# Rebuilding the quantised attention product of a two-product kernel: column term on TensorE, all four context groups converted before a block's tiles are evicted

## The chip, the cores and the metric

One NeuronCore of a Trainium2 chip runs the whole program. The metric is the device time of one execution in microseconds (us), as the median of several runs. Lower is better. The cores' engines are named as in the profile: PE (TensorE), DVE (VectorE), ACT (ScalarE), POOL (GpSimd) and SP (SyncE, which here only issues DMAs).

## What is computed

For two batches of 1024 tokens with 2048 features each, and a context matrix of 2048 x 2048 per batch:

```
q(v, s, z) = (clip(round(v / s + z), 0, 255) - z) * s
x = x + q(layernorm(x), s1, z1) @ q(ctx, s2, z2)                 # first product
y = layernorm(x)
base  = y @ kernel + bias
A_eff = einsum('bn,nri->bri', gate, lora_A);  B_eff = einsum('bn,nor->bor', gate, lora_B)   # b = 8 groups, n = 16, r = 32
delta = (y @ A_eff.T) @ B_eff.T + (y @ lora_A_shared.T) @ lora_B_shared.T                   # per group of 256 tokens
x = x + base + delta                                             # second product
```

## The kernel before

**Tiles and blocks.** A batch is 8 tiles of 128 tokens (`t`), its 2048 output columns are 4 blocks of 512 (`j`), and the 16 slices of the inner dimension are 4 groups of 4 (`g`). A PSUM bank holds one tile of one block. The program is written by hand, engine by engine, with semaphores; each engine works its own list in order, so the order of the code is the order of the work. Batch 0 runs its first product (blocks 0 to 3), then its second, then batch 1 the same.

**First product.** Both operands are whole numbers in bf16. A context group is 1 MB of fp32: SP loads it into one of two halves of `stage` (L318), which it may do when the group two before has been converted; ACT scales it (L617), DVE rounds it (L1159) and writes it centred into `ring` (L1163, `converted`). `ring` has room for two blocks here. `lhs` holds the quantised and transposed tokens. PE multiplies tile by tile (L841, 16 matmuls a tile); DVE evicts a tile with `evict1` (L1202), which adds it to `x2`. Because the operands are centred, each output needs a term per row and one per column. The row term is added by ACT (`row_terms`, L767). For the column term DVE sums the converted groups (L1175, L1180, L1183), PE sums that over the partitions with a matrix of ones (L853, or L860 for the very first block), ACT copies it out (`column`, L757) and POOL adds it to each tile of `x2` (`adjust`, L477). `evict1` waits for `adjusted`.

**In the first product of batch 0** the low-rank matrices are made too. `a_effective` (L889, 64 fp32 matmuls, printed as 128 records) follows block 0 on PE, `b_effective` (L903, 16 fp32 matmuls) comes ahead of block 3, and ACT copies their results out (L692, L720). DVE finds their largest magnitudes, and those of the first block of `kernel`, to choose powers of two as scales.

**Second product.** `norm2` (L1220) writes the normed tile, ACT and DVE split it into two fp16 parts in `hl` (`split_hi`, `low2` L1226) and SP transposes both into `lhs` (`turn_y`, L310 and L312). PE starts with tiles 0 and 1 together (`base0_pair`) and takes three matmuls a slice (L961 to L963). `lora_in` (L984), `product_p` and `delta` (L972, L973) add the low-rank part. DVE runs `norm2`, `low2` of tile after tile; in batch 0 two `max_of_w` of block 1 (L1339) stand ahead of tile 6's `norm2`, and their loads stand in SP's list behind `load_a(2)`, which waits for `lora_in(1)`.

**Between the batches** the tokens of batch 1 are normed and quantised during batch 0's second product and written to `q_scratch`. In the last block ACT issues their transposes (`turn_next`, L605), each when PE has done with that tile of `lhs`, and `ring` gets free group by group. In this block DVE runs `evict2` of tiles 0 to 4, context groups 0 and 1, tiles 5 to 7, context groups 2 and 3.

## Time and profile before

| | |
|---|---|
| Time, median of 3 runs | 1163.47 us (1163.18 to 1165.22) |
| Profiled execution, its own time | 1165.81 us |
| Its span, first to last instruction | 1164.2 us |
| PE busy | 1013.1 us (87%) |
| DVE busy | 599.5 us (51%) |
| ACT busy | 323.7 us (28%) |
| POOL busy | 247.6 us (21%) |
| Mean granted PE clock | 0.943 of 2.4 GHz |

PE is the engine to watch: the product matmuls are most of the span, and the time to win is where PE stands still or runs at the lower of its two clocks. A matmul of 512 columns shows some 0.38 us in the rows but starts 0.216 us after the one before; 0.43 us at the lower clock.

### The profile page before, as it was taken

What the parts mean: (1) busy time and instruction counts of PE and PEld (TensorE: products, weight loads), DVE (VectorE), ACT (ScalarE), POOL (GpSimd) and SP (SyncE); (2) the same over time, 40 slices, a digit from 0 to 9 for tenths busy, and PEclk for the clock granted to TensorE, in tenths of its full rate; (3) what the DMA queues carried; (4) which work ended last, traced back from release to release, by engine and by line L of the source; (5) the groups of instructions that cost most, each with busy time, mean ns of one, the idle gap of its engine ahead of it and who ended that gap; (6) DMA issues with size and microseconds to landing.
All of it is one profiled execution on the core that took longest, in us unless ns stands there. A gap on an engine that the chain in (4) does not pass through costs nothing.

```text
span 1164.2 us, 12162 instructions
## 1 busy us (share of the span) xinstructions
PE 1013.1 (87%) x4663; PEld 475.3 (41%) x4663; DVE 599.5 (51%) x786; ACT 323.7 (28%) x303; POOL 247.6 (21%) x246
## 2 busy tenths in 40 slices
PE   0388795778968999899999599998999999999995
PEld 0138342233525444344444244444554444444442
DVE  4952775898754546456441567798745114014010
ACT  1872545332210213213211244442213003003000
POOL 1030303351000130140150044440110301301200
PEclk9895797898988999999999799999999999999998
DMA  8872275545664731741759843356683305204010
GB/s 344 246 212 73 73 278 237 150 126 159 131 155 147 260 137 68 248 180 69 233 205 282 251 160 137 134 118 164 136 216 120 125 24 163 76 31 149 9 45 18
DMA packets 131736, 177.24 MB, mean 152 GB/s; under 512 B 104816, under 2 KB 104816, under 8 KB 119408
## 3 DMA queue, kind: packets, MB, share of 16 engines
q1 hardware_dynamic: 102000, 117.99, 34.3%
q0 software_dynamic: 11904, 50.34, 12.4%
q10 hardware_dynamic: 17792, 8.39, 2.9%
q8 instruction: 24, 0.39, 0.1%
q14 instruction: 16, 0.13, 0.0%
HBM read 124.26 MB, written 27.26 MB: 130 GB/s over the span
## 4 chain that ended last, share of the span: by engine, by line
PE 47%; DVE 22%; DMA 9%; ACT 8%; issue 8%; POOL 2%; ACTq 1%; SPq 1%; DVEq 0%; POOLq 0%
PE psum L961 13%; PE psum L962 13%; PE psum L963 13%; DVE stage L1159 4%; DVE ring L1163 3%; ACT x L767 3%; PE psum L984 3%; PE psum L889 2%; DMA xn<-in_x 2%; DMA stage<-in_w 2%; DVE x L1202 2%; DMA bias_sb<-in_bias 2%; POOL x L494 2%; DVE stats L1119 2%; ACT stage L617 2%
## 5 line engine op out<-in xcount | busy, mean ns | idle before, releaser
L961 PE MATMUL psum<-ring,lhs 128*128 128x512 f16 x1024 | 389.9, 381 | 21.8 <-DMA lhs<-hl 16.6
L962 PE MATMUL psum<-ring,lhs 128*128 128x512 f16 x1024 | 389.8, 381 | 0.0
L963 PE MATMUL psum<-ring,lhs 128*128 128x512 f16 x1024 | 389.5, 380 | 0.0
L841 PE MATMUL psum<-ring,lhs 128*128 128x512 bf16 x1024 | 236.0, 392 | 67.9 <-DVE ring L1163 57.1
L841 PEld LDWEIGHTS psum<-ring,lhs 128*128 128x128 bf16 x1024 | 101.6, 100 | 199.2 <-DVE ring L1163 60.8
L961 PEld LDWEIGHTS psum<-ring,lhs 128*128 128x128 f16 x1024 | 100.5, 98 | 145.3 <-issue 19.5
L963 PEld LDWEIGHTS psum<-ring,lhs 128*128 128x128 f16 x1024 | 100.6, 98 | 121.9 <-issue 1.9
L962 PEld LDWEIGHTS psum<-ring,lhs 128*128 128x128 f16 x1024 | 100.5, 98 | 120.4 <-issue 1.4
L1233 DVE SCALAR_TENSOR_TENSOR x<-psum,sc,x 128x512 f32<-128x512 f32 (+1 forms) x64 | 45.4, 747 | 182.3 <-PE psum L973 181.4
L494 POOL TENSOR_TENSOR x<-x,bias_sb 128x512 f32<-128x512 f32 (+1 forms) x64 | 88.5, 1407 | 216.0 <-DVE xn L1220 139.3
L624 ACT ACTIVATE ring<-stage,sc 128x2048 f16<-128x2048 f32 x32 | 63.6, 2000 | 214.1 <-PE psum L963 161.2
L1189 DVE SCALAR_TENSOR_TENSOR ring<-stage,sc,ring 128x2048 f16<-128x2048 f32 x32 | 74.8, 2349 | 78.4 <-ACT ring L624 78.2
L1159 DVE TENSOR_SCALAR stage<-stage 128x2048 f32<-128x2048 f32 x32 | 50.4, 1574 | 82.5 <-ACT stage L617 82.5
L617 ACT ACTIVATE stage<-stage,sc 128x2048 f32<-128x2048 f32 x32 | 65.9, 2086 | 81.7 <-DMA stage<-in_ctx_in 43.0
L500 POOL DMA_DIRECT2D out<-x x48 | 26.6, 554 | 243.5 <-DVE x L1233 238.9
L477 POOL TENSOR_TENSOR x<-x,xn 128x512 f32<-128x512 f32 x32 | 48.3, 1542 | 105.5 <-ACT x L767 98.4
L477 POOL TENSOR_TENSOR x<-x,bias_sb 128x512 f32<-128x512 f32 x32 | 44.5, 1423 | 87.8 <-ACT x L767 87.8
L612 ACT ACTIVATE hl<-xn 128x2048 f16<-128x2048 f32 x16 | 30.6, 1910 | 81.5 <-DVE xn L1220 70.2
L1195 DVE SCALAR_TENSOR_TENSOR b_st<-stage,sc,b_st 64x1024 f16<-64x1024 f32 x16 | 22.8, 1426 | 51.1 <-ACT b_st L631 51.1
L1202 DVE SCALAR_TENSOR_TENSOR x<-psum,sc,x 128x512 f32<-128x512 f32 x64 | 44.8, 743 | 3.5 <-POOL x L477 3.5
L1163 DVE TENSOR_SCALAR ring<-stage 128x2048 bf16<-128x2048 f32 x32 | 44.6, 1393 | 3.2 <-DVE stage L1159 0.5
L1339 DVE TENSOR_REDUCE sc<-stage 128x1 f32<-128x2048 f32 x16 | 36.0, 2278 | 17.3 <-DMA stage<-in_w 17.3
(128 smaller groups left out, 708.8 us busy)
## 6 DMA issues: line engine op xcount, KB each, us to landing
stage<-in_w SPq DMA_DIRECT2D x40, 1024.0 KB, 6.2
stage<-in_ctx_in SPq DMA_DIRECT2D x32, 1024.0 KB, 4.9
out<-x POOLq DMA_DIRECT2D x64, 256.0 KB, 3.6
x<-in_x POOLq DMA_DIRECT2D x8, 1024.0 KB, 14.9
xn<-in_x POOLq DMA_DIRECT2D x8, 1024.0 KB, 7.5
x<-in_x POOLq DMA_DIRECT2D x4, 2048.0 KB, 13.1
lhs<-in_lora_a SPq DMA_DIRECT2D x4, 1024.0 KB, 6.5
lhs<-in_lora_b SPq DMA_DIRECT2D x4, 1024.0 KB, 8.1
```

Source lines behind the costliest of these rows:

```text
L477: pool.tensor_tensor(v, v, col_sb[n % 2], ALU.add).then_inc(adjusted, 1)
L494: pool.tensor_tensor(v, v, bias_sb[:, :], ALU.add).then_inc(biased, 1)
L617: act.activation(s, s, ACT.Relu, bias=Z2, scale=IS2).then_inc(act_conv, 1)
L624: act.activation(ring[:, g, 0, :, :], stage[:, i % 2, :, :], ACT.Copy, scale=of_block(CW0, j)).then_inc(act_conv, 1)
L841: last = pe.matmul(psum[:, t, :], lhs_q[:, k, t * P:(t + 1) * P], ring_q[:, g, j % 2, u, :], start=(k == 0), stop=(k == KT - 1))
L961: pe.matmul(psum[:, t, :], hi, ring[:, g, 0, u, :], start=(kk == 0), stop=False)
L962: pe.matmul(psum[:, t, :], hi, ring[:, g, 1, u, :], start=False, stop=False)
L963: last = pe.matmul(psum[:, t, :], lo, ring[:, g, 0, u, :], start=False, stop=False)
L1159: dve.tensor_scalar(s, s, 255.0, ROUND, ALU.min, ALU.add).then_inc(dve_mid, 1)
L1163: dve.tensor_scalar(ring_q[:, g, j % 2, :, :], s, -(ROUND + CENTRE), None, ALU.add).then_inc(converted, 1)
L1189: dve.scalar_tensor_tensor(out=ring[:, g, 1, :, :], in0=stage[:, half_w(b, g), :, :], scalar=of_block(CW0, j), in1=ring[:, g, 0, :, :], op ...
L1202: dve.scalar_tensor_tensor(out=v, in0=psum[:, t, :], scalar=S12, in1=v, op0=ALU.mult, op1=ALU.add).then_inc(evicted, 1)
```

## The change

**Column term.** POOL's `adjust` is gone. ACT (`column`) and DVE (`column_low`) write the column sums as two fp16 parts into `col_parts`, and PE adds them in PSUM with one more matmul per tile (`column_term`). Tiles 0 to 3 get theirs together after tile 3, in block 0 of batch 0 tiles 0 to 4 after tile 4. Only with it is `psum_full` raised. `evict1` now waits for the row term instead of `adjusted`. In batch 0 the row terms of blocks 1 to 3 are one ACT instruction per tile.

**Low-rank matrices.** Half of `a_effective` runs ahead of block 0, the other half and all of `b_effective` right behind it. Their results go through DRAM scratch (`store_a_part`, `load_gates`); the part for the four gates of a batch is made in block 1 of that batch. The weights of the first block of `kernel` are loaded into free slots of `lhs` for their maxima (`max_of_first_w`).

**Start.** The scales and the gate come in one DMA. Context groups 2 and 3 of block 0 ("head" groups) have buffers of their own, in both batches, and do not use `stage`.

**Orders.** DVE converts all four groups of the next block and then evicts the tiles of this one; `ones`, `turn_next` and the head loads move as the diff shows (`turn_next` from ACT to SP). In batch 0's second product the loads for the two maxima of block 1 come right behind `turn_y(4)`.

```diff
             sp.wait_ge(x_in[1], 16)
-            load_ctx(0, 0, [0, 1])
+            load_ctx(0, 0, [0])
+            load_lora_a(0)
+            load_ctx(0, 0, [1])
+            load_head(0, 2)
+            load_lora_a(1)
+            load_head(0, 3)
             turn_q(0)
             turn_q(1)
-            load_ctx(0, 0, [2, 3])
+            load_lora_a(2)
+            sp.dma_start(ash(0), lora_as).then_inc(sh_in, 16)
             turn_q(2)
             turn_q(3)
-            sp.dma_start(ash, lora_as).then_inc(sh_in, 16)
-            load_lora_a(0)
-            load_lora_a(1)
+            load_lora_a(3)
+            turn_q(4)
+            turn_q(5)
             load_ctx(0, 1, [0, 1])
-            for t in range(4, TILES):
-                turn_q(t)
-            load_lora_a(2)
-            load_lora_a(3)
+            turn_q(6)
+            turn_q(7)
+            load_lora_b(0)
+            load_lora_b(1)
             load_ctx(0, 1, [2, 3])
-            load_ctx(0, 2, range(NG))
+            load_lora_b(2)
+            load_lora_b(3)
             sp.wait_ge(sh_in, 16)
+            sp.wait_ge(csum_full, 1)
             sp.dma_start(bsh, lora_bs.rearrange("r (a o) -> (r a) o", a=P // RANK)).then_inc(sh_in, 16)
-            for c in (0, 1, 3):
-                load_lora_b(c)
+            load_ctx(0, 2, [0, 1])
+            load_gates(0)
+            load_ctx(0, 2, [2, 3])
+            load_first_w(0)
+            load_first_w(1)
             load_ctx(0, 3, range(NG))
-            for n in range(2):
-                sp.wait_ge(a_dram[n], 16 * (NGATE // 2))
-            load_lora_b(2)
+            load_first_w(2)
+            load_first_w(3)
+
+            def turn_next(b, t):
+
+                if t < 2:
+                    sp.wait_ge(turned[t % 2], turns1(b, t) - 16)
+                else:
+                    sp.wait_ge(turned[t % 2], turns1(b, t - 2))
+                sp.wait_ge(base_done, TILES * blk2(b, 0) - TILES + t + 1)
+                sp.dma_start_transpose(lhs_q[:, :, t * P:(t + 1) * P], q_scratch[t]).then_inc(turned[t % 2], 16)
...
-                    load_ctx(b, 0, range(NG))
+                    load_ctx(b, 0, [0, 1])
+                    sp.wait_ge(q_rows, (b + 1) * TILES)
+                    load_head(b, 2)
+                    for t in range(2):
+                        sp.wait_ge(turned[t], turns1(b, t) - 16)
+                    load_head(b, 3)
+                    for t in range(TILES):
+                        turn_next(b, t)
+                    load_gates(b)
                     with sp.Fori(1, NBLK) as j:
-                        ctx_block(b, j, grp1(b, 0, 0), j * NG + grp1(b, 0, 0))
-                else:
-                    w_peaks_block(0)
...
                 turn_y(b, 4)
+                if b == 0:
+                    w_peaks_block(1)
                 load_a(b, 2)
                 turn_y(b, 5)
-                if b == 0:
-                    w_peaks_block(1)
...
-            def adjust(b, j):
-
-                n = b * NBLK + j
-                pool.wait_ge(col_ready, n + 1)
-                for t in range(TILES):
-                    pool.wait_ge(with_row, n * TILES + t + 1)
-                    v = x2[:, t, j * NW:(j + 1) * NW]
-                    pool.tensor_tensor(v, v, col_sb[n % 2], ALU.add).then_inc(adjusted, 1)
...
+                act.wait_ge(rows_ready, b + 1)
+                if b == 0:
+                    ctx_block(b, 1, [0, 1])
+                    row_terms(0, 1)
+                    column(0)
+                    ctx_block(b, 1, [2])
+                    for k in range(2 * KC, 3 * KC):
+                        a_eff_out(k)
+                    ctx_block(b, 1, [3])
+                    for k in range(3 * KC, KT):
+                        a_eff_out(k)
+                    for n in range(8):
+                        b_eff_out(n)
+                    row_terms(1, NBLK)
+                else:
+                    ctx_block(b, 1, [0])
+                    column(0)
+                    ctx_block(b, 1, [1])
+                    act.wait_ge(res_in[0], 16)
+                    row_terms(0, 1)
+                    ctx_block(b, 1, [2, 3])
+                for j in range(1, NBLK):
+                    if j < NBLK - 1:
+                        ctx_block(b, j + 1, [0])
+                    column(j)
+                    if j < NBLK - 1:
+                        ctx_block(b, j + 1, [1])
                     if b:
                         act.wait_ge(res_in[j], 16)
-                    for t in tiles:
-                        if j == 0:
-                            act.wait_ge(rows_ready, TILES // 2 + b if b else t // 2 + 1)
-                        v = x2[:, t, j * NW:(j + 1) * NW]
-                        act.activation(v, v, ACT.Identity, bias=RC[:, t:t + 1]).then_inc(with_row, 1)
-
-                for j in range(NBLK):
-                    column(j)
-                    row_terms(j)
-                    if b == 0 and j == 2:
-                        shared_hi()
-                        for g in range(NGATE):
-                            gate_hi(g)
-                    if j + 1 < NBLK:
-                        ctx_block(b, j + 1, [0, 1])
-                    if b == 0 and j == 0:
-                        for k in range(KT):
-                            a_eff_out(k)
-                    if j + 1 < NBLK:
+                        row_terms(j, j + 1)
+                    if j == 1:
+                        shared_hi(b)
+                        gate_hi(b, 0)
+                        gate_hi(b, 1)
+                    if j < NBLK - 1:
                         ctx_block(b, j + 1, [2, 3])
-                    if b == 0 and j == 2:
-                        for n in range(NBLK * NQ):
-                            b_eff_out(n)
+                    if j == 1:
+                        gate_hi(b, 2)
+                        gate_hi(b, 3)
...
+            def column_term(b, j, tiles):
+
+                n = b * NBLK + j
+                pe.wait_ge(col_ready, n + 1)
+                for t in tiles:
+                    pe.matmul(psum[:, t, :], ones[:, :], col_parts[:, n % 2, :], start=False, stop=True).then_inc(psum_full, 1)
...
             def first_block():
 
                 half = TILES // 2
+                a_effective(0)
+                a_effective(1)
                 for g in range(NG):
-                    pe.wait_ge(converted, grp1(0, 0, g) + 1)
+                    ring_ready(0, 0, g)
                     for t in range(half):
                         if g == 0:
                             tile_start(0, 0, t)
                         group1(0, t, g)
-                first_column_sum()
+                column_sum(0, 0)
                 for t in range(half, TILES):
                     tile_start(0, 0, t)
                     for g in range(NG):
                         group1(0, t, g)
+                    column_term(0, 0, range(half + 1) if t == half else [t])
+                a_effective(2)
+                a_effective(3)
+                for n in range(8):
+                    b_effective(n)
...
                         group1(j, t, g)
-                    if t == 0:
+                    if t == (0 if j else 2):
                         column_sum(b, j)
+                    if t >= TILES // 2 - 1:
+                        column_term(b, j, range(t + 1) if t == TILES // 2 - 1 else [t])
...
+            def column_low(b, j):
+
+                n = b * NBLK + j
+                v = col_parts[P // 2:P, n % 2, :]
+                dve.wait_ge(col_hi, n + 1)
+                dve.scalar_tensor_tensor(out=v, in0=psum[P // 2:P, CB, :], scalar=D1[P // 2:P, :], in1=v,
+                                         op0=ALU.mult, op1=ALU.subtract).then_inc(col_ready, 1)
...
             def evict_and_convert(b, j):
 
+                last_first = 4 if b == 0 and j == 0 else 0
+                if j == 0:
+                    row_terms(b)
                 ctx_group(b, j + 1, 0)
+                column_low(b, j)
                 ctx_group(b, j + 1, 1)
-                for t in range(4):
+                for t in range(last_first):
                     evict1(b, j, t)
-                ctx_group(b, j + 1, 2)
-                for t in range(4, 6):
+                if j == 1:
+                    shared_low(b)
+                    gate_low(b, 0)
+                    gate_low(b, 1)
+                for g in range(2, NG):
+                    ctx_group(b, j + 1, g)
+                if j == 1:
+                    gate_low(b, 2)
+                    gate_low(b, 3)
+                for t in range(last_first, TILES):
                     evict1(b, j, t)
-                ctx_group(b, j + 1, 3)
-                for t in range(6, TILES):
-                    evict1(b, j, t)
...
                 for j in range(NBLK - 1):
-                    if b == 0 and j == 2:
-                        power_a()
-                        a_low()
                     evict_and_convert(b, j)
                     if b == 0 and j == 0:
-                        peak_a()
+                        peak_a(2)
+                        peak_a(3)
+                        peaks_a()
+                        power_a()
+                        peaks_b()
+                    if b == 0 and j == 1:
+                        max_of_first_w(0)
+                    if b == 0 and j == 2:
+                        for g in range(1, NG):
+                            max_of_first_w(g)
+                        all_of_w(0)
+                        power_b()
 
                 j = NBLK - 1
-                if b == 0:
-                    peaks_b()
-                    max_of_w(0, 0)
-                    max_of_w(0, 1)
                 early_stats2(b, 0)
+                column_low(b, j)
                 evict1(b, j, 0)
                 late_stats2(b, 0)
                 if b == 0:
-                    max_of_w(0, 2)
+                    product_scale(0)
+                early_stats2(b, 1)
+                norm2(b, 0)
                 evict1(b, j, 1)
-                norm2(b, 0)
-                stats2(b, 1)
-                if b == 0:
-                    max_of_w(0, 3)
-                    all_of_w(0)
+                late_stats2(b, 1)
                 low2(b, 0)
...
+                    for t in range(2):
+                        evict2(b, NBLK - 1, t)
+                    for g in range(2, NG):
+                        head_group_mid(b + 1, g)
+                    for t in range(2, 5):
                         evict2(b, NBLK - 1, t)
                     for g in range(2):
                         ctx_group(b + 1, 0, g)
-                    for t in range(5, TILES):
+                    evict2(b, NBLK - 1, 5)
+                    for g in range(2, NG):
+                        head_group_end(b + 1, g)
+                    for t in range(6, TILES):
                         evict2(b, NBLK - 1, t)
-                    for g in range(2, NG):
-                        ctx_group(b + 1, 0, g)
+                    for g in range(NG):
+                        add_group(b + 1, 0, g)
```

Three places in the lists of the engines show what moves.

PE, batch 0, block 0 and what follows it, before (`pats_sb` is the gate pattern, so these rows are `a_effective`):

```order
L841 MATMUL psum<-ring,lhs 128x512 x64
L860 MATMUL psum<-ring,ones_b 128x512 x16
L841 MATMUL psum<-ring,lhs 128x512 x64
L889 MATMUL psum<-pats_sb,lhs 128x64 x64
L841 MATMUL psum<-ring,lhs 128x512 x16
```

And of the change (L1001 is `a_effective`, L978 `column_term`, L1015 `b_effective`):

```order
L1001 MATMUL psum<-pats_sb,lhs 128x64 x32
L943 MATMUL psum<-ring,lhs 128x512 x64
L969 MATMUL psum<-ring,b_st 128x512 x16
L943 MATMUL psum<-ring,lhs 128x512 x16
L978 MATMUL psum<-bias_sb,ones 128x512 x5
L943 MATMUL psum<-ring,lhs 128x512 x16
...
L1001 MATMUL psum<-pats_sb,lhs 128x64 x32
L1015 MATMUL psum<-lhs,pats_sb 128x512 x16
```

Half of `a_effective` stands first, `b_effective` has come forward from block 3, and behind tile 4 PE needs the column sums before it may go on to tile 5.

DVE, batch 0, the stretch in which block 2 is evicted and block 3 converted, before:

```order
L1159 TENSOR_SCALAR stage<-stage 128x2048
L1163 TENSOR_SCALAR ring<-stage 128x2048
L1175 TENSOR_TENSOR xn<-ring 128x2048
L1202 SCALAR_TENSOR_TENSOR x<-psum,sc,x 128x512 x4
L1159 TENSOR_SCALAR stage<-stage 128x2048
L1163 TENSOR_SCALAR ring<-stage 128x2048
L1175 TENSOR_TENSOR xn<-xn,ring 128x2048
L1202 SCALAR_TENSOR_TENSOR x<-psum,sc,x 128x512 x2
```

And of the change, from the second group on (L1353 is `evict1`):

```order
L1279 SCALAR_TENSOR_TENSOR bias_sb<-psum,sc,bias_sb 64x512
L1293 TENSOR_SCALAR stage<-stage 128x2048
L1297 TENSOR_SCALAR ring<-stage 128x2048
L1326 TENSOR_TENSOR xn<-ring 128x2048
...
L1326 TENSOR_TENSOR xn<-xn,ring 128x2048
L1331 TENSOR_TENSOR xn<-xn 128x1024
L1334 TENSOR_TENSOR xn<-xn 128x512
L1353 SCALAR_TENSOR_TENSOR x<-psum,sc,x 128x512 x8
L1513 TENSOR_REDUCE sc<-lhs 128x1 x3
```

The eight evictions have moved behind the last conversion and the sums; a new small instruction (L1279, `column_low`) stands behind the first conversion.

SP, batch 0's second product, between the transposes of tiles 4 and 5, before:

```order
L310 DMA_TRANSPOSE lhs<-hl 128x16x128
L312 DMA_TRANSPOSE lhs<-hl 128x16x128
L402 DMA ap_st<-a_scratch 128x2048
L310 DMA_TRANSPOSE lhs<-hl 128x16x128
L312 DMA_TRANSPOSE lhs<-hl 128x16x128
L370 DMA stage<-in_w 128x2048 x2
```

And of the change (L449 loads the weights, L481 is `load_a`):

```order
L338 DMA_TRANSPOSE lhs<-hl 128x16x128
L343 DMA_TRANSPOSE lhs<-hl 128x16x128
L449 DMA stage<-in_w 128x2048 x2
L481 DMA ap_st<-a_scratch 128x2048
L338 DMA_TRANSPOSE lhs<-hl 128x16x128
L343 DMA_TRANSPOSE lhs<-hl 128x16x128
```

The two weight loads have moved ahead of `load_a(2)` and of tile 5's transposes.

## Rows read from the trace of the kernel before

**Rows 1.** The page's first line

```profile
span 1164.2 us, 12162 instructions
```

**Rows 2.** Stages: us, busy of PE, PEld, DVE, ACT, POOL, clock, DMA share, GB/s

```profile
0.00:38.50 38.50, 0.00 (x0) 0.00 (x0) 20.95 (x55) 14.44 (x12) 5.34 (x16) 1.00 0.84 300
38.50:84.30 45.80, 36.34 (x144) 14.70 (x144) 31.40 (x55) 37.24 (x33) 8.37 (x7) 0.89 0.88 257
84.30:120.40 36.10, 27.54 (x128) 27.39 (x129) 9.58 (x9) 9.75 (x17) 3.44 (x2) 0.54 0.17 60
...
187.10:225.70 38.60, 18.47 (x33) 5.25 (x34) 30.03 (x29) 17.97 (x22) 17.28 (x13) 0.73 0.60 204
...
253.70:266.60 12.90, 0.00 (x0) 0.01 (x1) 12.14 (x14) 5.26 (x4) 4.53 (x2) 0.66 0.59 102
...
651.50:697.80 46.30, 32.81 (x135) 13.58 (x134) 27.80 (x27) 17.84 (x15) 13.82 (x11) 0.82 0.65 210
...
727.90:757.90 30.00, 28.14 (x130) 12.39 (x129) 22.64 (x22) 13.74 (x13) 11.84 (x8) 1.00 0.40 144
...
785.90:789.60 3.70, 0.05 (x1) 0.00 (x0) 3.70 (x3) 0.00 (x0) 0.00 (x0) 1.00 0.86 155
```

**Rows 3.** PE's waits: releaser, us in total, times, longest

```profile
PE psum L841 <- DVE ring L1163: 57.1, 7, 38.5
...
PE psum L972 <- DVE ap_st L1248: 16.5, 3, 13.5
```

**Rows 4.** DVE at the start: start us, us, instruction, [idle before]

```profile
14.01 0.06 DVE L1068 MEMSET sc<- 128x1 f32 x1 [14.01 <-DMA sc<-in_z]
```

**Rows 5.** DMA issues by line: KB each, median us from issue to landing

```profile
stage<-in_ctx_in SPq DMA_DIRECT2D x32, 1024.0 KB, 4.9
...
lhs<-hl SPq DMA_TRANSPOSE x40, 4.6
...
pats_sb<-in_gate SPq DMA_DIRECT2D x1, 4.0 KB, 1.8
```

**Rows 6.** PE in order of time, batch 0 and the start of batch 1

```profile
92.15 27.54 PE L889 MATMUL psum<-pats_sb,lhs 128*128 128x64 f32 x128 [7.92 <-DVE x L1202]
...
198.93 12.58 PE L903 MATMUL psum<-lhs,pats_sb 128*64 128x512 f32 x24 [11.92 <-DVE x L1202]
...
664.49 1.89 PE L841 MATMUL psum<-ring,lhs 128*128 128x512 bf16 x4 [11.09 <-DVE ring L1163]
```

**Rows 7.** DVE in order of time, batch 1, block 1

```profile
718.61 2.72 DVE L1202 SCALAR_TENSOR_TENSOR x<-psum,sc,x 128x512 f32<-128x512 f32 x4
721.25 1.22 DVE L1159 TENSOR_SCALAR stage<-stage 128x2048 f32<-128x2048 f32 x1
...
723.84 1.23 DVE L1175 TENSOR_TENSOR xn<-xn,ring 128x2048 f16<-128x2048 f16 x1
```

**Rows 8.** ACT in order of time, batch 1, block 1

```profile
702.31 5.00 ACT L767 ACTIVATE x<-x,sc 128x512 f32<-128x512 f32 x8
...
722.61 2.10 ACT L617 ACTIVATE stage<-stage,sc 128x2048 f32<-128x2048 f32 x1 [1.72 <-DMA stage<-in_ctx_in]
```

**Rows 9.** DVE in order of time, batch 0's second product

```profile
330.76 2.29 DVE L1339 TENSOR_REDUCE sc<-stage 128x1 f32<-128x2048 f32 x1 [12.08 <-DMA stage<-in_w]
```

**Rows 10.** SP's DMA issues in order of time: the start, and batch 0's second product

```profile
11.25 0.80 SPq L318 DMA_DIRECT2D stage<-in_ctx_in  x2
...
311.41 1.99 SPq L312 DMA_TRANSPOSE lhs<-hl  x1
...
324.82 1.61 SPq L370 DMA_DIRECT2D stage<-in_w  x2
```

**Rows 11.** ACT's DMA issues between the batches

```profile
648.31 11.39 ACTq L605 DMA_TRANSPOSE lhs<-q_scratch  x2
```

**Rows 12.** DVE in order of time, batch 1, block 3

```profile
764.64 0.75 DVE L1202 SCALAR_TENSOR_TENSOR x<-psum,sc,x 128x512 f32<-128x512 f32 x1 [0.20 <-POOL x L477]
...
782.58 2.40 DVE L1226 TENSOR_TENSOR hl<-xn,hl 128x2048 f16<-128x2048 f32 x1
```

534 lines of the change are left out of this document (309 added, 225 removed).

## The prediction

> **What bounds the kernel now.** I read the page's first line [rows 1], then windows at the stage boundaries [rows 2], then PE's waits [rows 3], then the timelines around them. In the second product PE runs at 0.216 us a matmul with few gaps; the time to win lies elsewhere. Batch 0's first product reaches from 38.5 to 266.6 us, 228 us, where 512 product matmuls are 110.5 us. The rest is: an idle start of 38.5 us, `a_effective` with the stall ahead of it (36.1 us in which PE is busy 27.5, at a clock of 0.54), `b_effective` with its stalls (38.6 us, of which PE is busy 18.5), and 12.9 us before the second product, when the clock has dropped as well [rows 2]. In batch 1, block 0 takes 46.3 us instead of 27.8, and a later block 30.0 [rows 2]. The largest waits are on DVE's conversions, and 13.5 us in one piece on `product_p` [rows 3].
>
> The base is the profiled execution, 1165.8 us with a span of 1164.2; it is 2.3 us above the median 1163.5, so I add 1165.8 - 1164.2 - 2.3 = -0.7 to a span. Times below are us from the span's start. The change is followed stage by stage, since in each the last wait is another.
>
> **Start.** DVE stands until 14.01, for a scale that lands late [rows 4]. One parameter DMA like the gate's, which took 1.8 us [rows 5], ends that wait; then x tile 1 binds, whose landing lets SP go at 11.25 [rows 10]. The first norm comes some 6.6 us earlier. Against that, SP now puts 6 MB (two context groups, two head groups, two `lora_a` parts) ahead of the first transpose, where it put 2 MB; with x that is 14.7 MB (14 of 1.05). The first stretch moved 300 GB/s at a DMA share of 0.84 [rows 2], so 357 if always busy: 41 us, ending near 44. I take the first transpose as held behind these loads, landing at 46 instead of some 36. ACT's quantising of tile 2 waits for it, and so do all later tiles.
>
> The Trainium skill, page "DMA: Bandwidth & Descriptors", section "Queues, rings and completion order", says that an engine takes one row's descriptors in ring order and alternates between rows. By that rule x on POOL's queue goes on while the transpose waits behind SP's loads; the sum would be the one I use.
>
> DVE's list then runs unbroken (statistics 2.5 a tile, conversions 1.2 + 1.2, `a_eff_out` and two maxima, some 6 in all, new here). Tile 7 is quantised near 84, when PE had finished block 0 before (84.3 [rows 2]). Now comes the new stall. The row terms wait for all 8 tiles; ACT then does two conversions (2.1 each), eight row terms (5.0) [rows 8] and `column`, DVE `column_low`: 84.4 + 4.1 + 5.0 + 0.7 + 0.5 = 94.7. PE, done with tile 4 near 75, waits there about 20 us. Five column terms, three tiles and their terms are 56 matmuls, 12.1 us, plus 2.3 at the lower clock: block 0 ends at 109 (before 84.3).
>
> **Low-rank work.** `a_effective` costs 0.215 us a record (27.54 / 128 [rows 6]); half of its 128 now run in the idle start, 64 remain: 13.8, to 123. `b_effective` is still 32 records at 0.524 (12.58 / 24 [rows 6], the first of them at the lower clock), 16.8 us; it waits some 1 us for tile 4's eviction, which is behind the fourth conversion, and ends near 140. Its ACT copies fall from 16 to 8. Block 1 starts at 140 and finds its groups converted.
>
> The Trainium skill, page "TensorE: Matmul & The Clock Gate", Part 1, says that activity releases the throttle. Busy 27.5 of 36.1 us these small matmuls sat at a clock of 0.54 [rows 2], so the row wins; at the full clock the 64 records would be 6.9 us, and the sum 7 less.
>
> **Blocks 1 to 3, batch 0.** A block is now 128 product matmuls, 8 column terms and a sum: 137 x 0.216 = 29.6 (64 terms in all, +13.8 us, where POOL's additions cost PE nothing by themselves). In block 1 ACT first does the wide row terms, 8 x 1.5 = 12.3 (three times 0.625, less overhead), then a conversion and `column`: col_ready at 157.9, when PE has waited 3.9. DVE does the low-rank parts of four gates between conversions (6 x 0.75), so its evictions start at 174.6; PE starts block 2 at 175.3 and waits 1.1 for the last eviction, as the column sum uses bank 7. Block 3 starts at 206 (before 225.7) and ends at 235.6.
>
> **Evict after all four conversions.** In a steady block started at T: conversion 0 by T+3.5, `column_low` T+5, conversion 1 T+9.4; groups 2 and 3 are loaded once 0 and 1 are converted (4.9 us to land [rows 5]), scaled (2.1 [rows 8]) and done with their sums by T+22.5. Eight evictions at 0.68 [rows 7] begin then; bank 0 is free at T+23.2 and PE wants it at T+29.6. The order alone costs nothing, with 6.4 us in hand. The 0.45 us of stall per block (30.0 against 29.6) goes.
>
> **Last block.** `column_term` holds the first `psum_full` until after tile 3, T+14.9, where the first eviction was at 764.64, T+6.7 [rows 12]. From there `norm2` and `low2` of two tiles are DVE work without a gap, 20 us (764.64 to 785.0 [rows 12]). So the second product starts at T + 14.9 + 20 + 4.4 for the transpose = T+39.2 instead of T+31.7 (757.9 to 789.6 [rows 2]); in batch 0, with the scale's small steps, T+40.5 = 246.5. **Batch 0's first product: -20.1 us** (266.6 to 246.5).
>
> **Second product, batch 0.** DVE waits 12.08 us for a weight load [rows 9] that SP issues at 324.82, though its buffer is free before. Behind tile 4's transpose (issued 311.41 [rows 10]) it lands by 319.6 and 322; two maxima end at 324.3 instead of 335.6, and `product_p` comes 11.4 earlier. PE's 13.5 us wait [rows 3] shrinks to 2.1, and with it go 2 us of lower clock: **-13.4**.
>
> **Batch 1.** The head groups are ready, so the 11.09 us wait of [rows 6] and two small ones after it, 13.5 in all, go. But PE comes to `column_term` at T+13.8, and col_ready needs ACT's `column`, which stands behind the first load of block 1. SP issues that load only after `turn_next(7)`, whose issue ended at 659.7 on ACT [rows 11], and the gate load: 661, landing with 2.3 MB at about 668.5, scaled 670.6, `column` 671.8, DVE's conversion and `column_low` 674. PE stops from 665.3 to 674, 8.7 us, and loses 2.3 at the lower clock. Block 0 becomes 40.4 instead of 46.3 (-5.9), blocks 1 and 2 -0.9, block 3 with its gap +7.3, clock +0.6: **+1.1**.
>
> Sum of the span: 1164.2 - 20.1 - 13.4 + 1.1 = 1131.8; less 0.7, 1131 us.
>
> **The rivals.**
> *The transposes are not held* (0.13). Plain rotation between transfers would land the first transpose at 34; median landing of transposes is 4.6 [rows 5], though none stood behind 4 MB. Everything up to block 3 comes 9 us earlier: 1122. The small records at the full clock (0.04) would give 1124.
> *More late loads* (0.17). The 168 us up to block 1 of batch 0 are a chain of ACT, SP and DVE with little slack; `load_lora_b(2)` blocks SP until `a_effective` is half done. If groups 2 and 3 and the gate load each come 5 us late, `b_effective` and block 1 move by 10, and batch 1's stall by 4: 1145. The DMA shares of 0.84 and 0.88 at the start [rows 2] speak for it, the shares of 0.17 to 0.6 later against.
> *Slower: the late evictions become the chain* (0.07). Place: each of five steady blocks. A conversion group late by L costs max(0, L - 6.4) per block, and the whole passes the gain of 33 from L = 13. That takes loads of 11 us instead of 4.9 for both pairs; DMA share is 0.40 there [rows 2], which speaks against. At L = 15 it gives 1131 + 43 = 1174.
> *The waits only move* (0.03): the 20 us stop after tile 4 grows to 50 as ACT's list is longer than I count, and 1163 comes out.
>
> **How the numbers follow.** My forecast (0.56) has a range of its own, 1122 to 1140: 5 us either way for the copy of `b_effective` and the clock, 4 for the start. With rivals 1 and 2 the range is 1116 to 1150. A measurement tells 0.2%, 2.3 us. Faster 0.90, within 0.03, slower 0.07.
>
> **What would show it.** Right: PE stops after tile 4 of block 0 for about 20 us on DVE's `column_low`; `a_effective` records at 0.215 us; evictions of a block in one run of eight that ends before PE needs bank 0; DVE's wait for the weight load under 3 us; a stop near 9 us at `column_term` in batch 1's block 0. Wrong: the first transpose landing before 38; a wait for `evicted` at tile starts in every block; base0 of batch 1 more than 42 us after block 3's start.

## The result, and the profile after

The changed kernel takes 1130.2 us (median of 4 runs, 1125.9 to 1131.7), the kernel before 1163.3: a ratio of 0.971, with an interval of 0.968 to 0.975. In a second job with six more runs it took 1131.8 us (1125.9 to 1134.0), ratio 0.9717 (0.9689 to 0.9745). The forecast was 1131, with a range of 1116 to 1150.

The profiled execution is the fastest of its kernel (1125.9 us). The top of its page:

```profile
span 1124.3 us, 12189 instructions
PE 1015.2 (90%) x4727; PEld 477.5 (42%) x4727; DVE 585.0 (52%) x794; ACT 310.9 (28%) x265; POOL 161.8 (14%) x187
```

PE's waits, to be read against [rows 3]: releaser, us in total, times, longest. The wait for `ring`, 57.1 us with the idle start in it, is gone: the idle start now stands in the first wait of `a_effective` (L1001), and the column's low half (L1279) is the new one. That on the product (L1095) has fallen from 16.5 to 6.0.

```profile
PE psum L978 <- DVE bias_sb L1279: 27.1, 3, 18.0
PE psum L1001 <- DMA lhs<-in_lora_a: 23.5, 1, 23.5
PE psum L1084 <- DMA lhs<-hl: 17.9, 2, 9.7
...
PE psum L1095 <- DVE ap_st L1405: 6.0, 3, 3.1
PE psum L943 <- DVE x L1353: 4.8, 2, 4.4
```

Windows by stage, columns as in [rows 2]: block 2 of batch 0; the gap before the second product; then batch 1's block 0 and its last gap.

```profile
175.50:206.70 31.20, 31.20 (x137) 13.76 (x138) 26.60 (x29) 7.18 (x5) 0.00 (x0) 0.95 0.31 119
...
236.40:246.10 9.70, 0.03 (x1) 0.01 (x1) 9.63 (x12) 1.51 (x2) 1.58 (x2) 0.70 0.72 145
...
617.40:654.20 36.80, 31.38 (x139) 13.55 (x136) 23.01 (x25) 15.84 (x14) 2.00 (x3) 0.95 0.85 285
...
744.00:752.20 8.20, 0.32 (x2) 0.00 (x0) 8.13 (x9) 0.26 (x2) 2.42 (x2) 0.80 0.85 162
```

The timeline of PE in batch 0's first product, with the idle time and its releaser in brackets. The 64 records of `a_effective` at 107.12 take 7.25 us; both `column_term` stops and the eviction wait at the start of block 2 are here. The last line is from batch 1: the column sum of its block 1 waits for the last eviction of block 0.

```profile
93.20 2.32 PE L978 MATMUL psum<-bias_sb,ones 128*128 128x512 f16 x5 [18.04 <-DVE bias_sb L1279]
...
107.12 7.25 PE L1001 MATMUL psum<-pats_sb,lhs 128*128 128x64 f32 x64
...
119.08 16.53 PE L1015 MATMUL psum<-lhs,pats_sb 128*128 128x512 f32 x32 [4.71 <-DVE x L1353]
...
153.62 1.04 PE L978 MATMUL psum<-bias_sb,ones 128*128 128x512 f16 x4 [3.97 <-DVE bias_sb L1279]
...
175.47 5.28 PE L943 MATMUL psum<-ring,lhs 128*128 128x512 bf16 x16 [4.45 <-DVE x L1353]
...
246.13 0.59 PE L1084 MATMUL psum<-ring,lhs 128*128 128x512 f16 x1 [9.69 <-DMA lhs<-hl]
...
658.91 0.38 PE L963 MATMUL psum<-xn,ones 128*128 128x512 f16 x1 [1.07 <-DVE x L1353]
```

By large stages, each from a timeline (starts of the first matmuls of a product):

| Stage | before | forecast | after | after, second profile |
|---|---|---|---|---|
| to batch 0's second product | 266.6 | 246.5 | 246.1 | 250.6 |
| second product, batch 0 | 384.9 | 371.5 | 371.3 | 374.4 |
| first product, batch 1 | 138.1 | 139.2 | 135.0 | 135.0 |
| second product, batch 1 | 374.6 | 374.6 | 371.8 | 372.5 |
| span | 1164.2 | 1131.8 | 1124.3 | 1132.4 |

Two profiles of the same kernel differ by 8 us, half of it before 250 us. So an effect below some 4 us is not told here from one profile of each kernel, unless two profiles agree up to the place of the edit.

### The profile page after: what moved, and what is told of

The parts are those of the page before. It is cut to its first block, busy times and chain, and to the rows that moved or that the text cites. A ratio compares the mean times of both kernels' runs of the same rounds, so it can differ in the third digit from the quotient of the medians.

```text
span 1124.3 us, 12189 instructions
## 1 busy us (share of the span) xinstructions
PE 1015.2 (90%) x4727; PEld 477.5 (42%) x4727; DVE 585.0 (52%) x794; ACT 310.9 (28%) x265; POOL 161.8 (14%) x187
## 3 DMA queue, kind: packets, MB, share of 16 engines
q1 hardware_dynamic: 119040, 126.64, 37.9%
## 4 chain that ended last, share of the span: by engine, by line
PE 60%; DVE 14%; DMA 10%; ACT 6%; issue 5%; SPq 3%; POOL 1%; DVEq 0%; POOLq 0%; ACTq 0%
PE psum L1084 15%; PE psum L1085 15%; PE psum L1086 15%; PE psum L943 11%; DMA stage<-in_w 2%; PE psum L1107 2%; DMA stage<-in_ctx_in 2%; ACT x L850 1%; DVE x L1353 1%; DVE stats L1245 1%; DVE ring L1340 1%; DMA lhs<-hl 1%; DMA bias_sb<-in_bias 1%; ACT stage L696 1%; SPq L333 1%
## 5 line engine op out<-in xcount | busy, mean ns | idle before, releaser
L1084 PEld LDWEIGHTS psum<-ring,lhs 128*128 128x128 f16 x1024 | 100.5, 98 | 143.8 <-issue 22.2
L943 PEld LDWEIGHTS psum<-ring,lhs 128*128 128x128 bf16 x1024 | 102.2, 100 | 138.9 <-issue 12.9
L586 POOL TENSOR_TENSOR x<-x,bias_sb 128x512 f32<-128x512 f32 (+1 forms) x64 | 91.3, 1452 | 187.8 <-DVE xn L1375 113.7
L696 ACT ACTIVATE stage<-stage,pats_sb,sc 128x2048 f32<-128x2048 f32 x28 | 58.2, 2087 | 57.8 <-DMA stage<-in_ctx_in 57.0
L1293 DVE TENSOR_SCALAR stage<-stage 128x2048 f32<-128x2048 f32 x28 | 34.3, 1225 | 44.0 <-ACT stage L696 43.8
L1353 DVE SCALAR_TENSOR_TENSOR x<-psum,sc,x 128x512 f32<-128x512 f32 x64 | 44.0, 743 | 14.5 <-PE psum L978 14.3
L1001 PE MATMUL psum<-pats_sb,lhs 128*128 128x64 f32 x128 | 21.4, 348 | 31.0 <-DMA lhs<-in_lora_a 23.5
L978 PE MATMUL psum<-bias_sb,ones 128*128 128x512 f16 x64 | 21.8, 414 | 27.1 <-DVE bias_sb L1279 27.1
L1218 DVE BATCH_NORM_STATS2 stats<-xn 128x6 f32<-128x512 f32 x32 | 19.8, 681 | 46.7 <-DMA xn<-in_x 46.6
L1383 DVE TENSOR_TENSOR hl<-xn,hl 128x2048 f16<-128x2048 f32 x16 | 36.7, 2292 | 6.7 <-DMA lhs<-hl 4.5
## 6 DMA issues: line engine op xcount, KB each, us to landing
x<-in_x POOLq DMA_DIRECT2D x4, 2048.0 KB, 13.8
```

The lines of the kernel that those rows point to most:

```text
L586: pool.tensor_tensor(v, v, bias_sb[:, :], ALU.add).then_inc(biased, 1)
L696: act.activation(s, s, ACT.Relu, bias=Z2, scale=IS2).then_inc(act_conv, 1)
L943: last = pe.matmul(psum[:, t, :], lhs_q[:, k, t * P:(t + 1) * P], ring_q[:, g, j % 2, u, :], start=(k == 0), stop=False)
L1084: pe.matmul(psum[:, t, :], hi, ring[:, g, 0, u, :], start=(kk == 0), stop=False)
L1293: dve.tensor_scalar(s, s, 255.0, ROUND, ALU.min, ALU.add).then_inc(dve_mid, 1)
L1353: dve.scalar_tensor_tensor(out=v, in0=psum[:, t, :], scalar=S12, in1=v, op0=ALU.mult, op1=ALU.add).then_inc(evicted, 1)
```

## Experiments

The time of the kernel before lies between 1161.8 and 1163.4 (medians) in the three jobs. Times are medians of 5 runs or more; "r" is the ratio to the kernel before, measured beside it, to be held against 0.9717. The changed kernel itself was measured again in the first job only, so for the other two the ratio is the safer comparison. The interval of an r is some 0.003 to either side, so a difference of two of them is known to about 5 us: a gain of 7 us is clear of that, one of 4 us is not and needs the traces beside it.

| Kernel | us | r, interval |
|---|---|---|
| changed kernel | 1131.8 | 0.9717, 0.9689 to 0.9745 |
| old interleaving in it | 1122.4 | 0.9653, 0.9630 to 0.9676 |
| weight loads late again | 1138.8 | 0.9793, 0.9769 to 0.9817 |
| last block's terms after tile 1 | 1125.6 | 0.9681, 0.9655 to 0.9707 |
| head loads behind two transposes | 1123.6 | 0.9682, 0.9656 to 0.9708 |
| batch 1's column first | 1128.9 | 0.9735, 0.9705 to 0.9764 |
| gates 2, 3 behind evictions | 1121.3 | 0.9657, 0.9628 to 0.9687 |
| the same, and 8 evictions in block 0 | 1122.0 | 0.9671, 0.9643 to 0.9699 |
| interleaving + column first | 1123.4 | 0.9653, 0.9620 to 0.9686 |
| five edits together | 1115.0 | 0.9583, 0.9552 to 0.9615 |
| kernel before, late evictions | 1182.1 | 1.0152, 1.0116 to 1.0187 |
| kernel before, early weight loads | 1150.9 | 0.9904, 0.9875 to 0.9933 |

The yardstick of the first job:

> The changed kernel itself once more, as the yardstick for the other kernels of this job: 1130 us, between 1126 and 1132, 0.971 of the kernel before. All theories expect the same.

It gave 1131.8 us, as all theories had it.

**1. The order of the title, undone.**

```diff
-                for g in range(2, NG):
-                    ctx_group(b, j + 1, g)
+                cuts = [last_first, last_first, TILES] if last_first else [4, 6, TILES]
+                for t in range(last_first, cuts[0]):
+                    evict1(b, j, t)
+                ctx_group(b, j + 1, 2)
+                for t in range(cuts[0], cuts[1]):
+                    evict1(b, j, t)
+                ctx_group(b, j + 1, 3)
...
-                for t in range(last_first, TILES):
+                for t in range(cuts[1], TILES):
                     evict1(b, j, t)
```

> VectorE's old interleaving put back into the changed kernel (four evictions behind conversion 1, two behind conversion 2, two behind conversion 3) in every block but the first of batch 0. Theory A (the late evictions cost nothing, 6.4 us in hand per block): within 2 us of the changed kernel, and PE's waits at tile starts stay near zero in both. Rival B (the late order brings something of its own, the folded sums 1.4 us earlier per block, since they no longer stand behind evictions): 1 to 2 us slower for each of five blocks, +5 to +9, seen as waits of PE on the column sum. Rival C (evicting late costs, because VectorE idles ahead of conversions): 3 to 8 us faster.

Measured 1122.4 us, 9.4 under the changed kernel by the medians and 7.4 by the ratios: the late evictions cost time. Only my rival C had that sign and size, and its reason (VectorE idle ahead of conversions) is not the one that experiment 2 finds. PE's waits of this kernel hold no line for an eviction at a tile start, and the span to the second product is 242.7 us instead of 246.1 and 250.6. Both profiles of the changed kernel have that wait, 4.45 and 4.54 us, at the start of block 2 in batch 0. At one more place, the start of block 1 in batch 1, they have a small one, 0.2 to 0.3 us at the tile and 1.07 at the column sum; the other blocks have none. So the question was whether the order costs at the one place or a little everywhere.

**2. One block or all?**

```diff
                 for g in range(2, NG):
                     ctx_group(b, j + 1, g)
-                if j == 1:
-                    gate_low(b, 2)
-                    gate_low(b, 3)
                 for t in range(last_first, TILES):
                     evict1(b, j, t)
+                if j == 1:
+                    gate_low(b, 2)
+                    gate_low(b, 3)
```

> In block 1 VectorE does the low parts of gates 2 and 3 behind its eight evictions instead of ahead of them; the rest is the changed kernel. Theory A (in that one block the late evictions are on the path, because VectorE waits for ScalarE's gate copies, which wait for stores of the first two, and only then evicts; it is not the order of conversions and evictions as such): PE's wait of 4.5 us for the eviction at the start of block 2 of batch 0 falls under 1, 5 to 7 us faster than the changed kernel, nearly all that the old interleaving brought (8.4 of 1131). Rival B (all steady blocks gain a little from the old order): at most 3 us faster here.

Measured 1121.3 us, 10.5 under the changed kernel by the medians and 7.0 by the ratios: theory A. Moving two short instructions brings all that the interleaving brought, as far as the intervals can tell, with the conversions still ahead of the evictions in every block. The timelines of the changed kernel, ACT and then DVE, show what stood there:

```profile
169.47 0.72 ACT L797 ACTIVATE lhs<-lhs,sc 128x512 f16<-128x512 f32 x1 [6.46 <-DMA a_scratch<-lhs]
173.12 0.72 ACT L797 ACTIVATE lhs<-lhs,sc 128x512 f16<-128x512 f32 x1 [2.93 <-DMA a_scratch<-lhs]
```

```profile
168.28 0.42 DVE L1334 TENSOR_TENSOR xn<-xn 128x512 f16<-128x512 f16 x1
170.22 0.75 DVE L1483 SCALAR_TENSOR_TENSOR lhs<-lhs,sc 128x512 f16<-128x512 f32 x1 [1.51 <-ACT lhs L797]
173.87 0.75 DVE L1483 SCALAR_TENSOR_TENSOR lhs<-lhs,sc 128x512 f16<-128x512 f32 x1 [2.90 <-ACT lhs L797]
174.66 5.36 DVE L1353 SCALAR_TENSOR_TENSOR x<-psum,sc,x 128x512 f32<-128x512 f32 x8
```

DVE has converted and folded by 168.7. Then it waits for ACT's high halves of gates 2 and 3, which wait for the stores of gates 0 and 1 (one buffer for two gates), and eight evictions stand behind. PE is done with the block at 171.0 and waits for the first of them. In the profile with the gates moved no eviction wait is left at that place. That profile and the second one of the changed kernel agree to 0.1 us up to the column term of block 1 (156.96 and 157.07), so they show the price. Block 2 starts at, in the changed kernel and then with the gates moved:

```profile
178.93 6.24 PE L943 MATMUL psum<-ring,lhs 128*128 128x512 bf16 x16 [4.54 <-DVE x L1353]
```

```profile
174.21 3.62 PE L943 MATMUL psum<-ring,lhs 128*128 128x512 bf16 x16
```

The first is 4.7 us later, and its 16 matmuls take 2.6 us longer, at the lower clock behind the stop. Block 3 starts 7.3 us later (211.11 and 203.78), and so does the second product (250.55 and 243.21). That is the whole of the 7.0 us.

**3. The same edit in the kernel before.**

```diff
                 ctx_group(b, j + 1, 1)
-                for t in range(4):
+                first = 4 if b == 0 and j == 0 else 0
+                for t in range(first):
                     evict1(b, j, t)
                 ctx_group(b, j + 1, 2)
-                for t in range(4, 6):
-                    evict1(b, j, t)
                 ctx_group(b, j + 1, 3)
-                for t in range(6, TILES):
+                for t in range(first, TILES):
                     evict1(b, j, t)
```

`early_stats2` also waits for its tile's eviction, as in the changed kernel.

> The kernel before with nothing but the title's edit: in every block but the first of batch 0 VectorE converts all four groups and then evicts eight tiles in one run (the statistics of the last block wait for their tiles' eviction, as in the changed kernel). Theory A (in a steady block there are 6 us in hand, and PE's waits of 1.4 us for the column sum and 0.45 us for the first conversion in each of the later blocks come from evictions standing ahead of the last group's sum): 4 to 9 us faster than the kernel before. Rival B (neither order matters): within 2.3 us. Rival C (the loads of the kernel before are late, and evictions behind them stop PE as in batch 1's block 0): slower by 3 to 8.

Measured 1182.1 us, 18.7 slower: further than even the slower rival. In the profiles 9.0 us of it stand ahead of batch 0's second product and 9.4 in batch 1's first. PE's timeline of this kernel shows the places. Ahead of `b_effective` it stops for 27.58 us. The kernel before stops there for 11.92 [rows 6] and, in the middle of `b_effective`, once more for 7.57 (last fence of the three), which is gone here, so the price of this place is 8.1 us and not the difference of the first two. At the start of later blocks it is some 4 us each:

```profile
217.32 16.66 PE L903 MATMUL psum<-lhs,pats_sb 128*64 128x512 f32 x32 [27.58 <-DVE x L1202]
```

```profile
704.07 5.31 PE L841 MATMUL psum<-ring,lhs 128*128 128x512 bf16 x16 [3.95 <-DVE x L1202]
...
738.44 5.21 PE L841 MATMUL psum<-ring,lhs 128*128 128x512 bf16 x16 [4.66 <-DVE x L1202]
```

```profile
219.09 5.87 PE L903 MATMUL psum<-lhs,pats_sb 128*64 128x512 f32 x8 [7.57 <-ACT ap_st L720]
```

The reason in the later blocks is in DVE's timeline of a batch 1 block that starts at 704.1, here, and of one that starts at 685.0 in the changed kernel, below it:

```profile
717.24 2.34 DVE L1159 TENSOR_SCALAR stage<-stage 128x2048 f32<-128x2048 f32 x1 [8.62 <-ACT stage L617]
...
737.63 4.69 DVE L1202 SCALAR_TENSOR_TENSOR x<-psum,sc,x 128x512 f32<-128x512 f32 x7
```

```profile
686.72 1.21 DVE L1293 TENSOR_SCALAR stage<-stage 128x2048 f32<-128x2048 f32 x1
...
707.25 4.70 DVE L1353 SCALAR_TENSOR_TENSOR x<-psum,sc,x 128x512 f32<-128x512 f32 x7
```

In the kernel before ACT takes the column and eight row terms ahead of the block's first conversion, so DVE converts from T+13.2 and evicts from T+33.6, when PE has wanted bank 0 at about T+29.6. The changed kernel's ACT puts conversion 0 first and its row terms behind conversion 1: DVE converts from T+1.7 and evicts from T+22.2. The 6.4 us in hand, forecast from T+23.2, are real there, and they are bought by the rest of the rebuilding; the late evictions use them up and add nothing. How much ACT's order buys and how much the missing additions of POOL was not tried apart: in the kernel before the first three instructions of DVE's conversions also take some 1 us longer each within those additions (last section). The stop ahead of `b_effective` has another chain, in which DVE does the low-rank parts before it converts and evicts.

**4. Batch 1's block 0.**

```diff
-                    ctx_block(b, 1, [0])
                     column(0)
+                    ctx_block(b, 1, [0])
                     ctx_block(b, 1, [1])
...
+                if b and j == 0:
+                    column_low(b, j)
                 ctx_group(b, j + 1, 0)
-                column_low(b, j)
+                if not (b and j == 0):
+                    column_low(b, j)
```

> In block 0 of batch 1 ACT and VectorE take the column (its copy and its low half) ahead of the first conversion of block 1, for whose load they stand idle. Theory A (the 5.1 us stop at the column term is the column queued behind a late load): the stop goes, and with it 0.5 to 1.9 us of matmuls at half the clock; 5 to 7 us faster than the changed kernel (1131). Rival B (evictions or the next conversions become late by as much): under 2 us.

Measured 1128.9 us, r 0.9735: no gain against 0.9717. The stop is gone from PE's timeline, and another of 6.88 us stands at the next block's start. PE, then DVE of this kernel:

```profile
655.26 5.57 PE L943 MATMUL psum<-ring,lhs 128*128 128x512 bf16 x16 [6.88 <-DVE x L1353]
```

```profile
645.68 1.23 DVE L1293 TENSOR_SCALAR stage<-stage 128x2048 f32<-128x2048 f32 x1 [5.92 <-ACT stage L696]
...
654.45 5.36 DVE L1353 SCALAR_TENSOR_TENSOR x<-psum,sc,x 128x512 f32<-128x512 f32 x8
```

DVE stands 5.9 us for a late group while tiles 0 to 3, whose sums are done, wait behind it: rival B. That looked like the price of the late evictions, so the two edits were tried together.

> Two edits in the changed kernel: the old interleaving of evictions and conversions, and in block 0 of batch 1 the column ahead of the first conversion. Apart, they gave -8.4 us and nothing; in the second a wait of 6.9 us for the evictions took the column's place at the start of block 1, since all eight stand behind a conversion whose load landed late. Theory A (the late evictions turned that load into PE's wait): with the interleaving the wait falls under 2 us, batch 1's first product takes some 129 us instead of 135, and the time is 4 to 6 us under the interleaving alone (1122.4). Rival B (the late load itself binds PE, through the next block's conversions): no gain over 1122, PE waits on VectorE's conversions instead.

Measured 1123.4 us against 1122.4 for the interleaving alone: rival B. PE now waits first for the conversion and then for the eviction, at the same place:

```profile
653.05 1.04 PE L943 MATMUL psum<-ring,lhs 128*128 128x512 bf16 x3 [4.01 <-DVE ring L1297]
...
656.91 0.59 PE L963 MATMUL psum<-xn,ones 128*128 128x512 f16 x1 [2.82 <-DVE x L1353]
```

As I read the timelines, the first two groups' loads set the pace in both orders. ACT waits for them until 631.3 and 636.4, T+14.4 and T+19.5 of this block, then come its row terms (5.0 us) and the last two groups, so DVE has converted the fourth only at 653.0. With the interleaving in both, batch 1's first product takes 135.9 us with the column first and 133.8 without: in these two profiles it costs 2 us.

**5. The weight loads of batch 0's second product.**

```diff
-                if b == 0:
-                    w_peaks_block(1)
                 load_a(b, 2)
                 turn_y(b, 5)
+                if b == 0:
+                    w_peaks_block(1)
```

> SP issues the two loads whose maxima VectorE takes in batch 0's second product behind the transpose of tile 5 again, as the kernel before does, instead of ahead of it; nothing else changes. Theory A (this one move is the whole gain of 13.4 us in the second product of batch 0): +13 us against the changed kernel, VectorE waits about 12 us for the load, PE about 13 us for the low half of the product. Rival B (the rebuilt first product changed VectorE's phase, so the load is only a part): +4 to +8. Rival C (hidden anyway): under +2.

Measured 1138.8 us, +7.0 (r +0.0076, 8.8 us): about what rival B says, and not theory A's 13. DVE's wait for the load, and PE's for the product, of this kernel:

```profile
309.98 2.29 DVE L1506 TENSOR_REDUCE sc<-stage 128x1 f32<-128x2048 f32 x1 [9.84 <-DMA stage<-in_w]
```

```profile
PE psum L1095 <- DVE ap_st L1405: 14.7, 3, 11.7
```

Against 6.0 us the wait is 8.7 longer, and that is the time. The opposite edit in the kernel before:

> The kernel before with nothing but the two weight loads of batch 0's second product issued ahead of tile 5's transpose instead of behind it. Undoing that move in the changed kernel cost 7.5 us. Theory A (the move is worth what the low half of the product waits for it, 8.6 us between the two profiles; the rest of the 13.6 us of this stage came from elsewhere): 7 to 10 us faster than before. Rival B (the whole 13.4 us as predicted): 12 to 14 us faster.

Measured 1150.9 us, 12.5 faster by medians, 7.8 to 14.5 by the interval, which doesn't tell the theories apart. Its profile does so better: the second product takes 373.3 us instead of 384.9, 11.6 less, and the wait falls from 16.5 [rows 3] to

```profile
PE psum L972 <- DVE ap_st L1248: 6.1, 3, 3.1
```

So the move is worth 10.4 us of wait and 1.2 besides in the kernel before, most of the 13.4 forecast. In the changed kernel its undoing costs less, as DVE's wait is 9.8 us there and not 12.1. Counted from the start of the second product, DVE comes to it at the same time (52.3 and 52.1 us), but SP issues the loads 1.8 us sooner (56.4 and 58.2) and they land 2.0 us sooner.

**6. The transposes at the start.**

```diff
-            load_head(0, 2)
             load_lora_a(1)
-            load_head(0, 3)
             turn_q(0)
             turn_q(1)
+            load_head(0, 2)
+            load_head(0, 3)
```

> At the start SP issues the two head-group loads (2 MB) behind the first two transposes instead of ahead of them. Theory A (the transposes are held behind what SP issued before them, and they set the pace of ACT and so of PE's 18 us stop): 2 MB at 357 GB/s are 5.9 us; ACT's wait for the first transpose falls from 8.2 to some 3 us, the stop at the column term ends 4 to 5 us earlier, and all of batch 0 with it: 4 to 6 us faster than the changed kernel (1131). Rival B (the transposes land no earlier, their place in SP's queue does not matter): within 1 us, and ACT's wait stays at 8. Rival C (the heads now come late and stop VectorE or PE instead): slower by up to 5.

Measured 1123.6 us, r 0.9682, faster by 4 us by the ratios and 8 by the medians; the intervals overlap, so the traces must decide. SP's issue rows and ACT's wait, here and (second fence of each pair) in the changed kernel:

```profile
27.28 10.70 SPq L333 DMA_TRANSPOSE lhs<-hl  x2
```

```profile
27.22 16.28 SPq L333 DMA_TRANSPOSE lhs<-hl  x2
```

```profile
38.30 2.00 ACT L667 ACTIVATE hl<-xn,sc 128x2048 bf16<-128x2048 f32 x1 [3.10 <-DMA lhs<-hl]
```

```profile
43.32 2.00 ACT L667 ACTIVATE hl<-xn,sc 128x2048 bf16<-128x2048 f32 x1 [8.17 <-DMA lhs<-hl]
```

Two megabytes fewer ahead of them bring the transposes through 5.6 us sooner; 2 MB at the 357 GB/s of the forecast are 5.9. The stop at the column ends at 89.1 instead of 93.2 (93.1 in the second profile). Theory A for the cause. How much of it reaches the end is less sure. Against the changed kernel's second profile, like this one the slowest run of its kernel, the second product starts 4.0 us earlier (246.57 and 250.55) and the span is 3.9 shorter. Against the first profile the gain is down to 0.6 us by the start of block 2, because PE waits 6.25 us at the column term of block 1 instead of 3.97.

**7. `b_effective`'s wait.** The gates' edit again, and `last_first = TILES` in place of 4 for block 0 of batch 0.

> Two edits in the changed kernel: gates 2 and 3 behind the evictions of block 1, and VectorE evicts all eight tiles of block 0 of batch 0 ahead of conversions 2 and 3, where it evicts four. Theory A (b_effective's 4.7 us wait is the eviction behind the fourth conversion, and with the wait in block 2 gone the gain is no longer taken back there): 4 to 5 us faster than the kernel with the gates moved alone. Rival B (ScalarE's row terms and the stores of b_effective set block 1's start of work, so the column term only waits longer): under 2 us.

Measured 1122.0 against 1121.3: rival B. The wait of 4.7 us is gone, and PE stops 6.70 us at the next column sum, for ACT's last copies of `b_effective`. They stand behind the fifth copy, which waits 12.7 us for the store of the first part. ACT and PE of this kernel:

```profile
134.94 1.09 ACT L809 ACTIVATE hl<-psum 128x512 f32<-128x512 f32 x2 [12.71 <-DMA bg_scratch<-hl]
```

```profile
138.62 0.58 PE L963 MATMUL psum<-xn,ones 128*128 128x512 f16 x1 [6.70 <-ACT hl L809]
```

**8. The gap before the second product.**

```diff
-                    if t >= TILES // 2 - 1:
-                        column_term(b, j, range(t + 1) if t == TILES // 2 - 1 else [t])
+                    first = 1 if j == NBLK - 1 else TILES // 2 - 1
+                    if t >= first:
+                        column_term(b, j, range(t + 1) if t == first else [t])
```

> In the last block of each first product PE adds the column terms of tiles 0 and 1 after tile 1 instead of after tile 3 (7.3 us earlier). Theory A (the gap of 9.7 and 8.2 us ahead of the second product is VectorE's unbroken chain of norms, started by tile 0's column term): the chain starts some 7 us earlier, the gaps fall to about 2.5 and 1.5 us, and with the clock that they cost the time is 13 to 16 us lower. Rival B (the chain waits for something else as well, tile 1's norm or the transposes): 4 to 8 us lower. Rival C (another term, the column sum's maxima or the row terms, comes late too): no change.

Measured 1125.6 us, 6.2 less (r -0.0036, 4.2 us, within the intervals): the size of rival B, but neither batch does what it says. Theory A holds in batch 1, where the first product takes 127.5 us instead of 135.0. In batch 0 rival C holds and nothing is gained (39.5 us from block 3's start to the second product, 39.4 in the changed kernel): the column comes late, behind DVE's maxima of the first weight block, and the gap becomes a stop. DVE and PE of this kernel:

```profile
218.28 2.29 DVE L1514 TENSOR_REDUCE sc<-lhs 128x1 f32<-128x2048 f32 x1 [2.64 <-DMA lhs<-in_w]
...
223.40 0.76 DVE L1280 SCALAR_TENSOR_TENSOR bias_sb<-psum,sc,bias_sb 64x512 f16<-64x512 f32 x1
```

```profile
224.21 1.03 PE L978 MATMUL psum<-bias_sb,ones 128*128 128x512 f16 x2 [6.63 <-DVE bias_sb L1280]
```

**9. Together.** The edits of 1, 4, 6 and 8, and in batch 0 `column_low` of the last block ahead of the maxima.

> All that the runs so far speak for, in the changed kernel: the old interleaving; batch 1's column ahead of the first conversion; the head loads behind the first two transposes; the last block's first column terms after tile 1; and in batch 0 the low half of the last column ahead of the maxima of the first weight block. Theory A (each lies on the path in another stage, so they add: 8 + 5 + 4 + 8 for the last block of batch 1 + 3 to 6 for that of batch 0): 1101 to 1105 us. Rival B (in batch 0 the gains run into VectorE's maxima or the loads of the first weight block, as the stop of 6.6 us showed in the run of the last block alone): 1108 to 1112.

Measured 1115.0 us (1114.1 to 1120.3), ratio 0.9583: the fastest kernel here, 48 us under the one before, yet above both ranges. Of the 27 to 31 us hoped for, 17 came (16 by the ratios). Batch 1's column brought nothing (4): that product takes 129.9 us, 2.4 more than in experiment 8. In batch 0 the second product still starts at 241.9, against 242.7 with the interleaving alone, behind a gap of

```profile
PE psum L1085 <- DMA lhs<-hl: 14.2, 2, 12.9
```

for its transposes (14.2 us in two pieces, the longest 12.9). Block 3 ends 3.9 us earlier than with the interleaving alone, and the gap is 3.1 longer. Rival B's mechanism is there: tile 0 has its column term at 206.4, but DVE is at the maxima and evicts it only at 216.9, of which it stands 2.7 us for a weight load, and its norms start from there:

```profile
211.82 2.29 DVE L1522 TENSOR_REDUCE sc<-lhs 128x1 f32<-128x2048 f32 x1 [2.71 <-DMA lhs<-in_w]
```

## Why the prediction was right, and where not

**The time** of 1131 is right to 1 us, and the large terms are right by themselves: -20.1 forecast for batch 0's first product and -20.5 in the first profile (-16.0 in the second), -13.4 and -13.6 (-10.5) for the second product. Within the first some steps were off against each other. Of the five signs named for being right, two came as named: PE's stop after tile 4 (18.0 us) and DVE's wait for the weight load (1.3 and 1.1 us). The stop in batch 1 came with 5.1 us instead of 9, the run of eight evictions ended in time in every block but one of each batch, and the records of `a_effective` were not at 0.215 us. None of the three signs of being wrong came.

**Start.** DVE's scale wait went, the transposes were held (ACT goes on at 43.3, forecast 46; experiment 6 shows what holds them), tile 7 is quantised at 82.4 (84), the column is there at 93.2 (94.7), and PE stopped 18.0 us (20).

**`a_effective`** was over-priced. I took 0.215 us a record, from 27.54 us for 128 at a clock of 0.50. The 64 records left took 7.25 us, 0.113 each, at the full clock, 6.6 us under my 13.8. I had put this at 4 in 100. What stands ahead differs: a stop of 7.92 us in the kernel before [rows 6], dense matmuls here. The rule of the Trainium skill, page "TensorE: Matmul & The Clock Gate", Part 1, that activity releases the throttle, came within 0.4 us of the number here (6.9) and had not in the kernel before. But the small matmuls released nothing in either kernel: here the dense ones ahead had the clock up when they began. No run moves these matmuls alone. Of the 6.6 us, 3.7 were lost at once, since `b_effective` waited 4.7 us for an eviction where I had 1.

**The late evictions "cost nothing".** For steady blocks this holds: evictions began at T+22.2, forecast T+22.5. It failed in block 1 of batch 0. The step "DVE does the low-rank parts of four gates between conversions (6 x 0.75)" priced six instructions and not what they wait for: gates 2 and 3 waited for stores, so evictions began at 174.66, the 174.6 of the forecast to the decimal, although the block had started 4.6 us earlier (135.4 instead of 140). The gain of the faster records was lost there, and two errors cancelled. That the stage came out within 0.4 us of the forecast in the first profile is luck. Experiments 1 and 2 show the price of the step, 7 us by the ratios: the wait of 4.5 and 2.6 of lower clock behind it. The medians say 9 and 10, across jobs in which the kernel before was not equally fast either. A second, small place is in batch 1 (1.2 to 1.4 us).

**Last block.** Forecast T+39.2 and T+40.5 to the second product; measured 37.9 (714.6 to 752.5) and 39.4 (206.7 to 246.1). Experiment 8 confirms the cause for batch 1; in batch 0 DVE's maxima bind beside it, which the forecast has not.

**Second product of batch 0.** As forecast: the wait went from 13.5 to 3.1 in its longest piece (2.1 forecast). Experiment 5 shows that the move of the loads alone gives 11.6 of the 13.6 in the kernel before, and 7 to 9 us when it is undone in the changed one.

**Batch 1.** The stop at `column_term` was forecast at 8.7 us and is 5.11 (3.98 in the second profile), as the load landed by 631.2, T+13.8, where I had T+17. Block 0 took 36.8 us, 40.4 forecast. Against the +1.1 forecast the stage gained 3. What I did not see is that this stop covers another: when it goes, the loads stop PE at the next block's start (experiment 4).

**The rivals.** The mechanism of the slower one exists: it is a part of what the same edit does in the kernel before (+18.7 in all), where the conversions end 11 us later in a block. The rebuilt order kept it out of the steady blocks here. That the transposes were not held is excluded by experiment 6. Batch 1's second product gained 2 to 3 us that I hadn't forecast, at 361.3 us busy as before. The gain lies wholly behind the last matmul: from there to the end of the span, where only the last evictions and stores are left, it is 12.1 us in the kernel before and 9.4 in both profiles of the changed one. Why was not tried.
